# Attention loop written out, with the shift transposed by TensorE and twelve spread load slots

## The reference

```
x = x + 0.5 * ffn(layernorm(x))       # relu^2 FFN, output turned into spike counts over 5 steps
x = x + attention(layernorm(x))       # 16 heads of width 16, rotary q and k, causal softmax
x = x + 0.5 * ffn(layernorm(x))

scores = einsum('bhsd,bhtd->bhst', q, k) * 0.25
probs  = softmax(where(causal, -inf, scores))
out    = einsum('bhst,bhtd->bhsd', probs, v) @ Wo.T + bo
```

## Time and profile before

| | |
|---|---|
| Median of 3 runs | 1605.16 us (1602.48 to 1610.64) |
| Profiled execution, its own time | 1608.4 us |
| Span of its trace | 1606.7 us |
| Granted clock of TensorE, mean | 0.904 of full speed |
| Busy | PE 86%, PEld 51%, DVE 71%, ACT 54%, POOL 14% |
| First FFN phase, until about | 360 us |
| Attention: first unit, first scores, last sums read | 409.4, 456.6, 1346.6 us |

### The profile page before, as it was taken

One profiled execution on the slowest core, in us unless ns is written; L12 is line 12 of the kernel. 1 busy time (PEld: TensorE's weight loads), 2 busy tenths in 40 slices (PEclk: granted clock), 3 DMA queues, 4 the chain that ended last, 5 costly groups with the idle time before them and its releaser, 6 DMA issues. The chain is left out here.

```text
span 1606.7 us, 27137 instructions
## 1 busy us (share of the span) xinstructions
PE 1381.6 (86%) x8384; PEld 821.8 (51%) x8384; DVE 1139.5 (71%) x2689; ACT 860.6 (54%) x1155; POOL 229.9 (14%) x206
## 2 busy tenths in 40 slices
PE   5988888750799999999999989999999976899997
PEld 5877777640443343343343333433433422799986
DVE  5666676821788888877887887888888930567675
ACT  5644444310036666655665665666666655466564
POOL 0012222346001011010010110110110101110100
PEclk9999999875568899997997999999999978899999
DMA  5113333437152062070080260440620002222312
GB/s 204 40 40 105 105 118 100 150 123 95 13 69 34 6 83 24 5 101 8 9 98 5 30 82 5 55 52 6 72 34 5 8 8 68 92 80 92 95 51 66
DMA packets 101898, 97.86 MB, mean 61 GB/s; under 512 B 46288, under 2 KB 85200, under 8 KB 100048
## 3 DMA queue, kind: packets, MB, share of 16 engines
q1 hardware_dynamic: 101744, 95.98, 29.0%
HBM read 57.15 MB, written 37.75 MB: 59 GB/s over the span
## 5 line engine op out<-in xcount | busy, mean ns | idle before, releaser
L1001 ACT ACTIVATE probs<-s_ps 128x1024 f32<-128x1024 f32 (+3 forms) x640 | 542.7, 895 | 327.7 <-PE s_ps L1133 326.4
L1112 PE MATMUL m_ps<-kT,qT 64*128 64x512 f32 (+3 forms) x1280 | 478.9, 478 | 112.9 <-DMA qT<-qkT_parts 55.9
L1026 DVE TENSOR_REDUCE maxes<-m_ps 128x1 f32<-128x512 f32 x768 | 490.8, 684 | 48.5 <-PE m_ps L1112 44.2
L1112 PEld LDWEIGHTS m_ps<-kT,qT 64*128 64x128 f32 x1280 | 217.2, 201 | 502.2 <-DVE maxes L1026 274.0
L1133 PE MATMUL s_ps<-qT,kT 64*128 64x512 f32 (+3 forms) x1280 | 327.3, 416 | 13.8 <-DMA qT<-shiftT 10.5
L1031 DVE CUSTOM_DVE_ANT_0 masked<-m_ps,mask_b 128x384 f32<-128x384 f32 (+3 forms) x512 | 238.3, 488 | 130.6 <-PE m_ps L1112 125.0
L1150 PE MATMUL o_ps<-probs,v_w 128*32 128x512 f32 (+3 forms) x2560 | 322.4, 578 | 0.2 <-POOL probs L974 0.2
L974 POOL TENSOR_SCALAR_AFFINE_SELECT probs<-probs 128x512 f32<-128x512 f32 x128 | 81.6, 637 | 851.8 <-ACT probs L1001 851.8
L1133 PEld LDWEIGHTS s_ps<-qT,kT 64*128 64x128 f32 x1280 | 164.2, 198 | 41.0 <-ACT probs L1001 25.0
L313 ACT ACTIVATE relu_a<-ups_a 128x512 f32<-128x512 f32 x64 | 38.1, 596 | 100.8 <-PE ups_a L562 99.9
L1150 PEld LDWEIGHTS o_ps<-probs,v_w 128*32 128x32 f32 x2560 | 51.9, 111 | 76.5 <-issue 58.9
(11 more groups left out here) (124 smaller groups left out, 1917.7 us busy)
## 6 DMA issues: line engine op xcount, KB each, us to landing
kT<-qkT_parts SPq DMA_DIRECT2D x48, 256.0 KB
qT<-qkT_parts SPq DMA_DIRECT2D x96, 128.0 KB
qkT_parts<-qk_hi_a SPq DMA_DIRECT2D x32, 256.0 KB, 3.0
qkT_parts<-qk_lo_a SPq DMA_DIRECT2D x32, 256.0 KB, 3.4
qT<-shiftT SPq DMA_DIRECT2D x512, 1.0 KB
xin_a<-in_x SPq DMA_DIRECT2D x8, 512.0 KB, 4.0
xres_a<-in_x SPq DMA_DIRECT2D x8, 512.0 KB, 4.9
x<-xsum_a SPq DMA_DIRECT2D x8, 512.0 KB, 3.2
```

The costliest lines, as they stand in the source:

```text
L1001: act.activation(probs[:, b % PBUF, 2 * hp:2 * hp + 2, off:CH], s_ps[hp][:, :, off:CH], ACT.Exp, scale=D ** -0.5)\
L1026: dve.tensor_reduce(out, m_ps[:, bank, 0:width], AX.X, ALU.max).then_inc(max_read, 1)
L1112: pe.matmul(m_ps[:, bank, 0:width], qT[of % 2][r0:r0 + HR, j, h // 2, t * P:(t + 1) * P], kT[of % 2][r0:r0 + HR, h // 2, k * CH:k * CH + w ...
```

## The change

Five things change, all in `attention_phase`.

1. The loop is gone. All 32 steps are written out, and every wait has a constant.
2. The shift is transposed by PE. `negparts` (128 x 32) goes through a transposing matmul with the identity (L1012 of the changed kernel) into the next bank of the ring, four units behind the last unit of the step; DVE copies it out (L957). `shiftT` then has whole rows, and 4 transfers for each step carry it. The three `negate` operations that are left stand behind one unit each for every step, the last of a group too, except behind the very last unit.
3. `att` has two buffers, each with a semaphore of its own.
4. The next group's loads are twelve pieces, one for each of its first twelve slots, ahead of that slot's shift and store. Its zeroing of the shift rows and `v_in` go first; in group 0's own load they go last.
5. `masked` has three buffers, and DVE no longer waits for its own earlier reads ahead of each masked maximum.

```diff
-            turn = [(dn, j) for dn in range(2) for j in range(NJ)][2:] + [(2, 0), (2, 1)]
-            body(0, 0, 0, False)
-            body(0, 0, 1, False)
-            with eng.Fori(0, PAIRS - 1) as i:
-                for dn, j in turn:
-                    body(i, dn, j, False)
-            for dn, j in turn[:-2]:
-                body(PAIRS - 1, dn, j, (dn, j) == (1, NJ - 1))
+        def steps():
+            return [(n, j) for n in range(GROUPS) for j in range(NJ)]
...
+                    last = max(i for i, (_, e) in enumerate(order) if e[0] == "unit" and e[1] == n and UNITS[e[2]][0] == j)
+                    after = [i for i, (_, e) in enumerate(order) if i > last and e[0] == "unit"][:4]
+                    at = after[-1] if after else last
+                    order.insert(at + 1, (order[at][0], ("shift", n, j)))
...
-                else:
-                    dve.wait_ge(neg_step, 3 * t + 3)
-                    wait(dve, shift_in, SHIFTS * t)
-                    dve.transpose(shiftT[:, :], negparts[:, :, :].rearrange("p a c -> p (a c)").bitcast(F32))\
-                       .then_inc(neg_out, 1)
+            def shift_out(e):
+                i = ITEM[e]
+                dve.wait_ge(max_done, i + 1)
+                wait(dve, shift_in, SHIFTS * step_no(e[1], e[2]))
+                dve.tensor_copy(shiftT[:, :], m_ps[0:2 * G * T, i % MB, 0:P]).then_inc(max_read, 1)
...
+            def turn_shift(e):
+                i = ITEM[e]
+                free_bank(i)
+                pe.wait_ge(neg_step, 3 * step_no(e[1], e[2]) + 3)
+                pe.transpose(m_ps[0:2 * G * T, i % MB, 0:P], negparts[:, :, :].rearrange("p a c -> p (a c)"), ident[:, :])\
+                  .then_inc(max_done, 1)
...
-                        for r in range(P // VW):
-                            c0 = VW * r + G * T * a + G * T // 2 * par
-                            sp.dma_start(out[:, :, r, :].bitcast(F32), shiftT[c0:c0 + G * T // 2, :]).then_inc(shift_in, 16)
+                        row, c0 = HR * par + KR + a, G * T * a + G * T // 2 * par
+                        out = qT[n % 2][row:row + 1, j, :, :].rearrange("o h (t q) -> o (h t) q", t=T)
+                        sp.dma_start(out.bitcast(F32), shiftT[c0:c0 + G * T // 2, :]).then_inc(shift_in, 16)
...
+            for n in range(GROUPS):
+                for x in range(BLOCKS):
+                    if n + 1 < GROUPS:
+                        if x == 0:
+                            wait(sp, s_done, 2 * block_no(n, 0, 0))
+                            wait(sp, v_ready, n)
+                            load_rest(n + 1)
+                        if x < len(TERMS):
+                            load(n + 1, *TERMS[x])
+                    moves(BLOCKS * n + x)
```

More of the change, by code:

```diff
@@ L764, in place_units @@
             return slots
[L766 to L781, removed]
@@ L864, in _, with moves @@
+            def moves(g):
+                for what, n, j in ITEMS.get(g, []):
+                    if what == "shift":
+                        shift(n, j)
+                    elif what == "sums":
+                        store(n, j)
             sp.dma_start(ident[:, :], w["ident"]).then_inc(const_in, 16)
@@ L867, in _ @@
             sp.dma_start(bias[:, :], w["bv"].partition_broadcast(P)).then_inc(bias_in, 16)
[L869 to L890, removed]
@@ L932, in _ @@
-            load(0, 0, range(NT))
-            for x in range(MAX_FROM, 0):
-                if x in out_slots:
-                    shift(0, 0, out_slots[x])
-            steps(sp, body)
-            sp.wait_ge(att_out, 16 * NJ * B * NG)
+            sp.wait_ge(ones_ok[0], 4)
+            for term in TERMS:
+                load(0, *term)
+            load_rest(0)
+            for g in range(MAX_FROM, 0):
+                moves(g)
+            sp.wait_ge(ones_ok[1], 4)
+            for n in range(GROUPS):
+                for x in range(BLOCKS):
[7 more added lines that the diff above has]
+                    moves(BLOCKS * n + x)
@@ L939, in _ @@
+            moves(BLOCKS * GROUPS)
+            for p in range(2):
+                sp.wait_ge(att_out[p], 16 * NJ * GROUPS // 2)
         @block.gpsimd
@@ L1094, in _ @@
-            for x in range(MAX_FROM, 0):
-                slot(0, 0, x, 0)
-            steps(dve, body)
+            pending = []
+            for g in range(MAX_FROM, BLOCKS * GROUPS + 1):
+                for e in ITEMS.get(g, []):
+                    if e[0] == "unit":
+                        unit(e)
+                        if LAST_UNIT[e[1], UNITS[e[2]][0]] == e:
+                            pending += [(e[1], UNITS[e[2]][0], k) for k in range(3)]
+                    elif e[0] == "shift":
+                        while pending:
+                            negate(*pending.pop(0))
+                        shift_out(e)
+                    else:
+                        normalise(e)
+                    if pending:
+                        negate(*pending.pop(0))
@@ L1184, in _, with ring @@
-            pe.wait_ge(const_in, 32)
-            for x in range(MAX_FROM, 0):
-                for u in unit_slots[x]:
-                    find(0, 0, x, 0, u)
-            steps(pe, body)
+            def ring(items):
+                for e in items:
+                    if e[0] == "unit":
+                        unit(e)
+                    elif e[0] == "shift":
+                        turn_shift(e)
+                    else:
+                        turn_sums(e)
+            pe.wait_ge(const_in, 32)
@@ new lines, in _ @@
+            for g in range(MAX_FROM, 0):
+                ring(ITEMS.get(g, []))
+            slots = [(n, j, b) for n, j in steps() for b in range(T * j + T)]
+            for g, (n, j, b) in enumerate(slots):
+                items = ITEMS.get(g, [])
+                units = sum(e[0] == "unit" for e in items)
+                q = [units * quarter // 4 for quarter in range(4)]
+                ring(items[:q[1]])
+                scores(n, j, b, 0)
+                ring(items[q[1]:q[2]])
+                scores(n, j, b, 1)
+                ring(items[q[2]:q[3]])
+                if g >= 2:
+                    products(*slots[g - 2])
+                ring(items[q[3]:])
@@ L1191, in build @@
+            for slot in slots[-2:]:
+                products(*slot)
+            ring(ITEMS[BLOCKS * GROUPS])
 def build(nc, x, w, out):
```

382 lines of the change are left out of this document (162 added, 220 removed).

## The result

The changed kernel takes 1545.66 us, the median of 4 runs (1544.93 to 1549.04), against 1603.82 us before in the same comparison; the ratio is 0.9635, 95% interval 0.9601 to 0.9668. I had forecast 1580 us with a range from 1565 to 1598. The sign was right; the gain is 58 us where I had 25, and the time lies outside the range. The profiled execution has a span of 1543.2 us (1606.7 before), so the trace shows the whole gain, 63.5 us between the two profiled executions.

The account below looks back on a forecast made before the run. PE was taken to bound the long middle, with DVE close behind. The terms summed to -24.9 us, taking the profiled 1608.4 to 1583.5, so a median of about 1580 us, with an 8-in-10 range of 1565 to 1598.

Parts of the forecast that it names:

- The start: Group 0's load: `v_in` moved behind all of q and k saves its 4.8 us; bounds 0 and 8.
- Jumps and registers: Written-out loop: two jumps back gone, -8.5, and cheaper steps without loop registers in six groups, -4.9.
- The rival of code fetch: Written-out code pays for its fetch as the loop did, so -8.5 and -4.9 fall away: 1593.4; chance 0.12.
- Sixteen transfers become four: Between step 3's shift and its first scores: the waits for the transfers in the middle go, -3.3; bounds 2 and 4.
- The row of DVE operations: Behind a group's last unit: one small operation stands instead of four, 0.4 us at seven places, -2.8; bounds 0 and 5.
- What is late next is PE's own queue: Behind a group's last unit: with DVE's row shortened, PE's own queue would be the next limit; no size given.
- Priced at nothing: Second `att` buffer, third `masked` buffer and spread of the loads: 0, with no wait showing on either buffer.
- The turned shift: Transposition as new work on PE, the bound engine: 0.2 us at 31 places, +6.2; bounds 4 and 13.
- The rival in which PE stands at the turn: PE waits for DVE's `negate` chain at every step: 1648; decides from 1.1 us a place; chance 0.04.
- The end: Behind the last unit: last shift's wait gone, -4.8, and 2 us of slow clock won back, together -6.8; bounds 2 and 10.
- The clock: Rival: 1 us of slow clock behind each of two jumps and eight group ends goes, 10 us more: 1570; chance 0.14.

Follow-up runs that it names:

- all but the turn: The whole change except the turned shift with its 4 transfers, the pieces of the loads and the second `att` buffer, against the kernel before: 1583.51 us, ratio 0.9859.
- The spread alone: Kernel before with only the three DVE operations behind each group's last unit set between the next group's first units: 1616.31 us, ratio 1.0053.
- last run: Changed kernel with the very last turned shift one slot later and every turn six units behind its step's last unit, not four: 1539.04 us, ratio 0.96.

## Why the prediction missed

*The start*: -4.8. From the phase's first memset to the first unit 45.8 us before, 40.9 now. The size is right, the mechanism in part: with `v_in` last but the zeroing of the shift rows still first (all but the turn) it was 43.2 us, so `v_in` brought some 2.6, and the rest goes with the order of the other transfers. The traces of the other kernels that start from the changed one have 39.8 to 41.9.

*Jumps and registers*: -13.4; alone, -18. Right in mechanism, somewhat small, with the clock's part left out. In the two steps that hold neither a jump nor a fall of the clock, 0 and 1, writing out took 9.68 to 9.57 us and 19.84 to 19.76. That is 0.19 in 29.5, an estimate of 0.7 for a group of 107 us, where I had 0.81. The rival of code fetch falls.

*Sixteen transfers become four*: -3.3, bounds 2 and 4. This is the step that failed. It took the waits that showed for the whole price. The runs show +45 for sixteen in the changed kernel, of which 6.5 are in the last group, 5 to 6 us in each other one, and 0 for eight. The same paragraph held the numbers: four blocks to cover sixteen transfers of 10.72 us and 1.1 to land. I called this just too short, compared it with blocks at their usual 2.7 us, and did not ask how long slots 20 to 23 really were. They took 14 us before, and the floor was 14 too: the two us before the issue begins belong to it. With both limits equal almost no wait shows. Nor are these blocks 2.7 us by themselves: their scores are 512, 384, 256 and 128 wide, and unhindered the four take 9.7 us, not 10.8. What made those four slots faster (the spread, and the semaphore step's part in them) was given back to the floor, and only with the floor gone does it count there. The spread alone, which I priced at -2.8, made the kernel slower.

*The row of DVE operations*: -2.8; +3 when undone in the changed kernel, and slower, not faster, when done alone in the kernel before. Right in size, but only without the floor and the step. "What is late next is PE's own queue" was wrong: next were the shift's transfers.

*Priced at nothing*: the second failure. With the third masked buffer the semaphore step went, and that was 14 us (two buffers without the step would have done: 1546.96 us). I wrote that no wait showed. None does: it is put down to PE, which really is waited for, only the idle time is 0.39 and not 0.21 us.

*The turned shift*: +6.2. PE's blocks with one are 0.1 to 0.5 us longer than in the kernel with all but the turn: slots 4 to 6 together 0.09, slot 31 0.09, slots 20 and 21 0.53. With what slots 2 and 39 differ, some 0.6 us a group, 5 in all. That leaves out the turn in slot 24, where the clocks of the two runs differ and where PE waits 0.5 us for the third operation in every group up to 6; moving the turns away from there (last run) brought 3.6 us. So the term was 5 to 9, within its bounds. The rival in which PE stands at the turn came true at ten places, 5.7 us in all, far from its point of decision. (That point was 1.26 us a place by the sum of 1580, not 1.1.)
The Trainium skill (VectorE: DVE Perf Modes, Rules for kernel authors) calls a 32 x 32 transposition fastest on DVE; here DVE's took 0.21 us and PE's 0.284, so the rows agree. It was the layout that the transposition on PE leaves, whole rows and so a quarter of the transfers, that was worth 45 us in the changed kernel.

*The end*: -6.8. Steps 2 and 3 of the last group, from the reading of the sums of its step 1 to that of its step 3, went from 1346.59 - 1279.83 = 66.8 us to 1282.79 - 1224.53 = 58.3, -8.5, with the 2 us for the late turn inside. Right.

*The clock*: a rival at 0.14 with 10 us. It did do better, by more than that: from 13 falls and 95.6 us on the lower level to 7 and 41.0, between 470 us and the last unit. Two falls stood at the loop's jumps and seven at the group ends, as the rival had it, and all nine are gone. What I had against it, that no row tied a fall to a gap of 1 us, was a row not looked up: behind each of the first seven groups' last units PE stood still for 0.86 to 1.08 us, and the clock fell each time. But the gain was not the clock's by itself, since the sixteen transfers held slots 20 to 23 at 14 us also where it stayed at full speed.

The prices above are each measured with the rest in place, in one kernel or the other, so they overlap and do not add up to the 58 us.

## What to carry to other kernels

A short wait can mean that two limits on the same stretch are equal, and not that either is cheap. For a chain that begins and ends at known places, add up its length and compare it with the stretch's real length. Where they agree, removing the other limit alone brings nothing there, or harm, as the spread alone did (ratio 1.0053), and the price of the chain shows only once the other limit is gone. The other order, four transfers in the kernel before with all else as it was, was not run. And look at a small group's idle time ahead of it, not only at who ended it: 0.39 beside 0.21 us for the same releaser was an extra instruction here.

## What the runs showed of the hardware

A semaphore step on DVE between a wait and the next operation put up to 0.18 us more between a matmul's end and DVE's start (0.21 in place of 0.03 in the rows above), at masked units that DVE was waiting for, though the step itself has no busy time in the profile. A wait alone in its place cost nothing measurable (1546.96 against 1545.66 us).

The granted clock fell at each standstill of PE of 4 to 5 us for the shift: in the changed kernel with 16 transfers it was at half speed for 13.7 us from there, seven times out of seven; in the other kernels for 3.4 to 17.1 us. It fell also at 13 of 14 group ends where PE stood still about 1 us and the semaphore step was there. In the changed kernel shorter falls stay, 3.4 or 6.8 us from slot 25 or 26 on, with no standstill longer than about 0.5 us there. The Trainium skill (Runtime: NRT & Kernel Launch, Instruction fetch mechanics) says that a taken branch out of the fetch window stalls; the two jumps, 4.24 us each and gone with the loop, agree.
